# New order tables, a swapped end and a split first load in a two-layer gated transformer kernel

## What is computed

```python
x = x + tanh(g_xattn[0]) * L0_xattn(layernorm(x), ctx)   # 16 heads of 16; q and k each go through a layernorm
x = x + tanh(g_ffn[0])   * L0_ffn(layernorm(x))          # three 256x256 products, then tanh
x = x + tanh(g_xattn[1]) * L1_xattn(layernorm(x), ctx)   # 8 heads of 64; keys of x and of ctx side by side
x = x + tanh(g_ffn[1])   * L1_ffn(layernorm(x))          # 8 experts, the best 2 of each token, weighted
# an expert:  (silu(t @ gate.T) * (t @ up.T)) @ down.T , added to its tokens' rows
```

## Time and profile before

| | us |
|---|---|
| median of the runs | 626.09 |
| the profiled execution | 626.46 |
| its span in the trace | 624.6 |
| PE busy, PEld busy | 589.4, 493.6 |
| DVE busy, ACT busy, POOL busy | 391.3, 308.8, 284.6 |
| POOL's powers (L1658), 16 | 87.0 |
| max0 (L1038), 32 | 55.0 |
| idle time of POOL ahead of L389, in all | 96.3 |

### The profile page before, as it was taken

One profiled execution on the slowest core, in us unless ns is written; L12 is line 12 of the kernel. 1 busy time (PEld: TensorE's weight loads), 2 busy tenths in 40 slices (PEclk: granted clock), 3 DMA queues, 4 the chain that ended last, 5 costly groups with the idle time before them and its releaser, 6 DMA issues.

```text
span 624.6 us, 13726 instructions
## 1 busy us (share of the span) xinstructions
PE 589.4 (94%) x5636; PEld 493.6 (79%) x5636; DVE 391.3 (63%) x769; ACT 308.8 (49%) x590; POOL 284.6 (46%) x240
## 2 busy tenths in 40 slices
PE   7789989999988999999999999999899999999994
PEld 6657667677666877878787888877789999989993
DVE  7563675686676555566656565566757777755751
ACT  2235545545554445454545455546436666646541
POOL 5957386577560036455455654651110443311324
PEclk9979999999998999999999999999999999999997
DMA  8900190000000000000000000008253776645212
GB/s 236 365 14 1 66 404 10 2 2 1 3 1 2 1 1 1 1 9 20 4 23 9 17 16 8 16 8 350 86 143 151 242 229 221 196 105 209 44 19 23
DMA packets 23787, 50.93 MB, mean 82 GB/s; under 512 B 7024, under 2 KB 16544, under 8 KB 20384
## 3 DMA queue, kind: packets, MB, share of 16 engines
q1 hardware_dynamic: 18400, 45.33, 20.2%
q0 software_dynamic: 4224, 3.70, 3.3%
q10 hardware_dynamic: 1088, 0.88, 0.5%
HBM read 37.89 MB, written 13.31 MB: 82 GB/s over the span
## 4 chain that ended last, share of the span: by engine, by line
PE 71%; POOL 14%; DVE 9%; issue 2%; ACT 2%; DMA 1%; POOLq 0%; DVEq 0%; ACTq 0%
PE ps L58 12%; PE ps L60 11%; PE ps L59 11%; POOL sr L1658 11%; PE ps L718 5%; PE ps L687 5%; PE ps L700 4%; DVE KN L1038 3%; PE ps L648 2%; PE ps L662 2%; PE ps L760 2%; PE ps L638 2%; PE ps L576 2%; PE ps L557 2%; PE ps L592 1%
## 5 line engine op out<-in xcount | busy, mean ns | idle before, releaser
L1700 POOL TENSOR_SCALAR P<-P,rinv 112x487 f32<-112x487 f32 x56 | 87.8, 1579 | 57.9 <-DVE rinv L1071 57.8
L1658 POOL TENSOR_TENSOR sr<-sv,mhalf 125x32 f32<-125x32 f32 x16 | 87.0, 5436 | 1.3
L58 PE MATMUL ps<-XGf,WH 128*128 128x256 f32 x256 | 72.6, 283 | 0.4 <-DVE XGf L1261 0.4
L60 PE MATMUL ps<-XGf,WL 128*128 128x256 f32 x256 | 72.5, 283 | 0.0
L59 PE MATMUL ps<-XGf,WH 128*128 128x256 f32 x256 | 72.4, 283 | 0.0
L389 POOL DMA_INDIRECT out<-WS,rows_i x16 | 28.6, 1786 | 96.3 <-ACT WS L1558 92.3
L1038 DVE TENSOR_REDUCE KN<-ps 112x4 f32<-112x1500 f32 x32 | 55.0, 1718 | 26.2 <-PE ps L557 26.1
L1339 DVE TENSOR_TENSOR WL<-WR,WH 128x1024 fp32r<-128x1024 f32 x48 | 57.2, 1221 | 13.6 <-ACT WH L1612 10.0
L1481 ACT ACTIVATE P<-ps,nm 112x487 f32<-112x487 f32 x64 | 42.0, 662 | 44.6 <-DVE nm L1063 40.0
L1432 ACT ACTIVATE P<-ps 125x1344 f32<-125x1344 f32 x32 | 41.3, 1292 | 42.4 <-PE ps L576 42.4
L1063 DVE TENSOR_REDUCE nm<-ps 112x1 f32<-112x487 f32 x64 | 39.4, 655 | 22.3 <-PE ps L687 22.3
(11 more groups left out here) (230 smaller groups left out, 1500.7 us busy)
## 6 DMA issues: line engine op xcount, KB each, us to landing
WR<-in_gupT SPq DMA_DIRECT2D x16, 1024.0 KB, 7.0
WR<-in_dwnT SPq DMA_DIRECT2D x8, 1024.0 KB, 10.4
xs<-ZT SPq DMA_DIRECT2D x14, 516.0 KB, 5.8
CT<-in_ctxT SPq DMA_DIRECT2D x1, 2250.0 KB, 10.9
P<-xs SPq DMA_DIRECT2D x8, 256.0 KB, 10.2
Wk<-in_L_xattn_Wk SPq DMA_DIRECT2D x2, 512.0 KB, 10.8
Wv<-in_L_xattn_Wv SPq DMA_DIRECT2D x2, 512.0 KB, 11.5
P<-xs SPq DMA_DIRECT2D x8, 128.0 KB, 2.7
```

Source lines behind the costliest of these rows:

```text
L58: e.matmul(out, ah, bh, start=start, stop=False)
L60: return e.matmul(out, al, bh, start=False, stop=stop)
L1658: e.tensor_tensor(sr[:, p, :], sv[:, p, :], mhalf[0:125, 0:32], ALU.pow).then_inc(s("sr"), 1)
L1700: e.tensor_scalar(P[:, k, 0:487], P[:, k, 0:487], rinv[:, k:k + 1], None, ALU.mult).then_inc(s("psc"), 1)
```

## The change

All entries of the tables that are not shown stay. Beside the times in them, the change writes the last expert's last quarters in another order, loads the second tile of the first expert by ACT's queue, and does the first gate product in a new function.

```diff
-QUAD = ((-0.75, "S0"), (0.52, "max0"), (3.51, "qt2"), ...
+QUAD = ((-0.75, "S0"), (0.45, "max0"), (3.51, "qt2"), ...
 FIRST = (
...
-         (-29, "wq")        (-16, "kp", 0, 0, 0)     (3.8, "kp", 1, 0, 1)     (4.9, "kq", 1, 0)     (9.2, "spk", 1, 1)
+         (-28.65, "wq")     (-17.9, "kp", 0, 0, 0)   (3.48, "kp", 1, 0, 1)    (4.58, "kq", 1, 0)    (8.96, "spk", 1, 1)
 PREP = (
...
-         (-37.87, "cs")     (-22.7, "kq", 0)
+         (-36.62, "cs")     (-22.35, "kq", 0)
 VALUES = (
...
-         (6.34, "vc", 0)
+         (6.38, "vc", 0)
 TAIL0 = (
...
-         (52.03, "norm", 1) (78.72, "rtanh")
+         (57.19, "norm", 1) (77.59, "rtanh")
 FIRST1 = (
...
-         (-11.6, "k1c", 0)  (-11.5, "k1", 1)         (-3.6, "q1c")            (-3.5, "v1", 0)       (-1.5, "v1", 1)
+         (-11.74, "k1c", 0) (-11.64, "k1", 1)        (-3.22, "q1c")           (-5.79, "v1", 0)      (-1.38, "v1", 1)
 PREP1 = (
...
-         (8.25, "k1c", 2)   (12.5, "k1c", 3)         (25.87, "v1c", 2)
+         (9.91, "k1c", 2)   (12.76, "k1c", 3)        (22.8, "v1c", 2)
 TAIL1 = (
...
-         (16.12, "res", 3)  (20.63, "norm", 3)       (23.31, "xtc", 3)        (28.05, "rt3")
+         (15.6, "res", 3)   (20.74, "norm", 3)       (22.25, "xtc", 3)        (28.62, "rt3")

 # tensor_experts, xin
-                        w.wait_ge(s(f"xg{j}"), 16 * (x // 2 + 1))
+                        if x == 0 and t_ == 1:
+                            w.wait_ge(s("xg_first"), 16)
+                        else:
+                            w.wait_ge(s(f"xg{j}"), 16 * (x // 2 + 1))
 # tensor_experts, up
+                    if u == 1:
+                        first_gate(e, w)
                     w.wait_ge(*pair_done("xin", x))
-                    for part in range(2):
+                    for part in range(u == 1, 2):
 # tensor_experts, down
+                    parts = ((dc, 0), (dc, 1))
+                    if (x, dc) == (NE - 1, 2):
+                        parts = ((2, 0),)
+                    elif (x, dc) == (NE - 1, 3):
+                        parts = ((3, 0), (2, 1), (3, 1))
+                    for dc, t_ in parts:
...
+        def first_gate(e, w):
+            gate = ps[:, PAIRS[1][0], :].rearrange("p (c n) -> p c n", c=2)
+            w.wait_ge(s("xina"), 1)
+            for c2 in range(2):
+                for k in range(2):
+                    o = k * 2048 + c2 * 128
+                    w.wait_ge(*split_done(0, o // 1024))
+                    for W in (WH[0], WL[0]):
+                        e.matmul(gate[:, c2, :], W[:, o:o + 128], XGT[:, 0, 0, k * 256:(k + 1) * 256],
+                                 start=(k == 0 and W is WH[0]), stop=False)
+                w.wait_ge(*pair_done("xin", 0))
+                for k in range(2):
+                    o = k * 2048 + c2 * 128
+                    t = e.matmul(gate[:, c2, :], WH[0][:, o:o + 128], XGT[:, 0, 1, k * 256:(k + 1) * 256],
+                                 start=False, stop=(k == 1))
+            t.then_inc(s("gate"), 1)
 # vector_experts, the scale of tile 0
-                    w.wait_ge(s("down"), 2 * (4 * x + 3) + 1)
+                    w.wait_ge(s("down"), 2 * (4 * x + 3) + (x < NE - 1))
 # scalar_experts, ahead of its list
-            w.wait_ge(s("rt4"), NB)
+            w.wait_ge(s("scatter"), 32 * NB)
+            e.dma_start(XG[:, 1, :], xs[128:256, 0:D]).then_inc(s("xg_first"), 16)
 # sync_experts, pair
-                    e.dma_start(XG[:, 2 * j:2 * j + 2, :],
-                                xs[x * NT:x * NT + 256, 0:D].rearrange("(t p) d -> p t d", p=128)).then_inc(s(f"xg{j}"), 16)
+                    n = 2 if x else 1
+                    e.dma_start(XG[:, 2 * j:2 * j + n, :], xs[x * NT:x * NT + 128 * n, 0:D].rearrange(
+                        "(t p) d -> p t d", p=128)).then_inc(s(f"xg{j}"), 16)
```

## The result

The changed kernel took 616.75 us (median of 4 executions, 615.44 to 617.50) beside 625.95 of the kernel before (625.69 to 626.26): a ratio of 0.9853, with an interval of 0.9837 to 0.9868. In a second set of five executions it took 615.57 beside 625.44: 0.9849 (0.9819 to 0.9879). The forecast was 618.7 and its range 616.8 to 621.8.

What follows compares the result with a forecast made beforehand. Bound: TensorE where full; in the first layer, a ring of scores, max0 and exponential delayed by DVE's wait for POOL. Terms 5.10 + 0.79 + 0.35 + 0.48 + 0.62 = 7.34 us gave 618.7, range 616.8 to 621.8.

Steps and rivals of the forecast that it cites:

- the clock step: Behind the fifth stretch the clock falls to half; the next round takes 5.85 us, not 5.06: 0.79 won.
- the start: Batch 0: max0 goes ahead of a weight split on DVE, 0.35 us won, between 0 and 0.74.
- the small terms: Moves taken as 0 us: others at the start, v1(0,0) and copies in the second layer, the split first load.
- The five stretches: First layer, once in each of five batches: max0 1.17 us earlier, less 0.15, so 1.02 each, 5.10 won.
- POOL's lock: First layer: ksc on DVE meets POOL's small steps for rstd, costing 0.15 us per stretch, at most 0.57.
- the rival built on it: First layer: rstd holds up DVE's second norm in all five stretches, each wins 0.45 us; 621.6, chance 0.22.
- the load in halves: Experts' first tokens: 256 rows loaded in halves on SP's and ACT's queues, 0 us, within 0.38 either way.
- The gate: First gate of the experts: four matmuls start on ACT's high part during the wait for DVE's low part, 0.48 us won.
- the end: Last expert: first tile ends 6 matmuls sooner (0.72 us), less than 0.1 lost; scale and scatter come 0.62 sooner.
- the rival of the falling clock: The clock falls all the same, near 185 us or in another thin stretch, losing 0.79 us: 619.5, chance 0.14.

Runs made afterwards that it cites:

- e1 to e3: The kernel before with norm(b,1) moved behind the next max0 and radd alone (623.41 us), cs moved behind ob alone (623.64), and both moves (618.34).
- e9: The kernel before, order untouched, with idle-time transposes added on TensorE at the start and in the fifth stretch: 623.46 us, ratio 0.9974.
- e10: The changed kernel, unaltered, in five more executions: 615.57 us, ratio 0.9849.
- e8: The changed kernel with 20 more small idle-time transposes on TensorE in the waits at the start: 615.17 us, ratio 0.9831.

## Why the prediction was wrong, step by step

The forecast was 618.7 and 616.75 was measured. In the profiled execution 8.90 us went where the sum had 7.34; of the 1.56 between them 0.68 is the clock step and 0.54 the start, the two terms that were sized wrongly, and the small terms and chance make up the rest.

**The five stretches** were right in size, 5.18 against 5.10, and right in their cause: e1 to e3 show that the norm is the wait that holds max0, and that cs is needed with it. But the term was put together wrongly. It took 1.17 for max0 and subtracted 0.15 for POOL's lock. max0 did come 1.17 sooner (6.91 to 5.74); the lock cost DVE nothing, since ksc takes 0.69 (0.68 before) and it is POOL's rstd that grows by 0.31. The 0.15 came from elsewhere: the next round takes 5.21 instead of 5.06, because st now stands behind TensorE's queue. Two errors of one size cancelled. By the rule of the Trainium skill (SBUF — State Buffer, Who interferes with whom) whoever issues second is blocked; the longer rstd agrees, and the rival built on it, in which rstd goes first, did not happen in any of the five: ksc starts 0.25 us ahead of it. POOL's first small step, which was to cost 0.15, does start ahead of ksc, by 0.05 to 0.14, but ksc takes only 0.01 more than before.

**The clock step failed.** "The next ring round, from 182.36 to 188.21, takes 5.85 in place of 5.06: 0.79 us ... I take the 0.79 as won." The half clock that the earlier trace rows show goes on to 191.6 (shown above), into the next round, which took 5.77: 0.78 + 0.69 = 1.47, and 1.47 is what went. The count stopped one round too early. The reading behind it was right as far as the runs go: e9 fills the wait, leaves the order as it was, and its profile has no half clock there.

**The start failed in its size.** "All other moves of the start stand behind POOL's powers: 0." The exchange of cs(2) with kss(1,0) does not stand behind a power, it stands ahead of one. The start gave 0.89 instead of 0.35 in the profiled execution, and gives 1.70 when the clock does not fall there (83.70 - 82.00).

**Small terms set to nothing** each paid a little: v1(0,0) 0.20, the load in halves 0.24 (453.07 - 450.49 = 2.58 in the changed kernel) to 0.30. The gate gave 0.54 (0.48 forecast), the end 0.66 to 0.70 (0.62). In the profiled execution chance added 0.67 behind the last scatter and took 0.98 in the second layer, by the half clock near 420, which the rival of the falling clock had at 0.79.

**The range failed for a reason of its own.** It was made of what could be off in the order, for an execution like the one profiled. The three times at hand lay within 0.45 us, and I took them for the kernel's. Over 69 executions the kernel before spans 6.5 us, and those with times like the three have granted clocks of 0.984 to 0.989, so all of them the half clock somewhere. A fall of the clock that the trace shows once should have been carried as a chance in every thin stretch, in both kernels, and not as a fixed term of one.

Compared without half clocks, by marks, the order is worth 1.70 + 5.18 + 0.20 + 0.8 + 0.65 = 8.5 us; the best executions of the kernel before and of e8, 622.41 and 614.50, are 7.9 apart. The rest of the measured 9.2 to 9.9 is put down to the clock: all five profiles of the old order with open waits have the fall near 185, none of the changed kernel has. How often executions that were not profiled have it is not shown. That part of the clock's gain, which the forecast has only as 0.79, and the start's gain are what the range left out; the time came out below it by 0.05.

## What to carry to other kernels

A wait that is taken away from the head of one engine's queue is worth only as much as the other engine's queue leaves: look from where the freed instruction's reader starts, and whether that reader waits for it or for its own queue; two edits may be worth nothing and half, and together the whole. An instruction that empties a shared PSUM bank has a second reader to look for: whoever is dealt that bank next. When a trace shows the clock down once, follow it to its end before pricing it, and count over how many executions it is there. An edit worth under half a per cent is read from marks in the traces, since the times of such a kernel spread by more.

## What was not expected of the hardware

Kernels with the same work on TensorE ahead of it (0.60 and 0.61 us in 3.10; 2.85 and 2.85 in 3.70) had the clock halved in one execution and not in the other; so had the changed kernel itself near 31 us, in its first profile and not in e10's. The Trainium skill, TensorE: Matmul & The Clock Gate, Part 1: The HAM clock gate, says that the hardware's look at TensorE's activity runs freely and does not start with the kernel, so that the same kernel may meet it differently; that would fit, and no run here shows it. None of the four profiles with idle-time transposes in the start's waits has the fall there, and in e8 they cost nothing (max0(3) at 46.64 beside 46.62); where they wait for a bank, as ahead of awT in e9, they only make the next instruction later, there by 0.39. And the last scatters' landing varied from 5.77 to 6.62 us over the profiles with nothing changed in them.
